# Layer 0: each group of four row transfers, from the fifth on, waits for one more convolution step

## The chip, the cores and the metric

The kernel runs on one core of a Trainium2 chip. The time is the device time of one execution, in microseconds (us). Of the kernel before there are three runs: median 1381.5 us, lowest 1380.76, highest 1385.48.

## What is computed

Four layers, each `x = x + attention(norm(x)) + ffn(norm(x))`, on x of 16 sequences x 256 tokens x 128 channels (4096 tokens). The change lies in layer 0, whose two parts are:

```
# attention part: a diagonal state-space scan, which is a causal convolution over time
y[b, t, d] = sum over s <= t of K[d, t - s] * xn[b, s, d]      K from log_A, B, C, D, log_dt
out_a      = xn + y @ W_out.T + b_out

# ffn part: a mixture of experts
probs      = softmax(norm(xf) @ gate_w.T)                      8 experts
w          = the two largest probs of each token, over their sum
out_f      = swiglu(xf, sWg, sWu, sWd)                         a shared expert, all tokens
           + sum over the two chosen experts e of w[e] * swiglu(xf, Wg[e], Wu[e], Wd[e])
swiglu(x, wg, wu, wd) = (silu(x @ wg) * (x @ wu)) @ wd
```

Layers 1 to 3 (two causal attentions with 16 heads, one windowed attention, three other feed-forward nets) are not touched.

## The kernel before

The work of an engine is a fixed program, written out by hand; engines wait for each other through counting semaphores. A layer ends with a barrier, so layer 1 starts when layer 0 is done. In layer 0 these pieces matter here:

- **The gate.** VectorE picks two experts for each token and works out `slot`: for choice n (0 or 1) and tile t (32 tiles of 128 tokens) the place of each token's row in the HBM array `expert_rows`, where the rows of one expert lie together. The array has two halves, for tiles 0 to 15 and 16 to 31.
- **The row transfers.** GpSimd (POOL) then issues 64 indirect DMAs from `send_rows` (L477), one for each tile and choice: 128 rows of `xn_tok`, 576 bytes each, go to their places. The order is: first half, choice 0 (16 transfers), then choice 1 (16), then the second half in the same way. Before choice 1 of a quarter (8 tiles) POOL waits for that quarter's choice 0 to have landed, moves the token numbers on (L473) and copies the second weight in (L474). Nothing else holds the transfers back: once `slots_ready` is there, POOL goes through all 64.
- **The convolution, beside it.** It has 16 steps of 8 channels. SyncE (SP) loads a step's Toeplitz matrices from HBM (`toeplitz`, L348, 1 MB) into one of four tiles; TensorE (PE) multiplies (`convolve`, L743 and L744, 32 matmuls, the last of which counts `c_mm` up by one); ScalarE (ACT) copies the result out of PSUM (`copy_y`, L572, which waits for `c_mm`); SP stores it (`store_y`, L353). A tile is loaded again for step s+4 only when `c_mm` says that step s is done.
- **The shared expert, beside it.** In the first 8 of the 16 steps PE also does one chunk of 512 tokens: `gate_up` (L708 to L710, 12 float16 matmuls), ahead of the convolution step, and `shared_down` (L726, 16 float32 matmuls) behind it. ACT does the silu (L558), VectorE (DVE) the product (L1067) and the sum into x (L1097). So a step is gate_up, convolve, shared_down in the first 8 steps, and convolve alone in the last 8.
- **The routed experts, after it.** When the convolution's results are stored, SP waits for the transfers of the first half (`wait_rows(0)`) and loads rows back, 512 at a time (a quad, L366); there are 20 quads. For each, PE turns the rows (L794), multiplies (L805 to L807, L726), and ACT scales the results (L606). POOL sends them with four indirect DMAs for each quad (`send_outs`, L492). The rows of the second half are waited for (`wait_rows(1)`) ahead of loading the eleventh quad.

The steps' waits on PE, and the loop of SP that follows them:

```
def convolve(step):
    a, w = step
    m = w % 2
    pe.wait_ge(t_in[w], a * 16 + 16)
    pe.wait_ge(u_taken, a * (2 * TW) + w * 2 + 2)
    pe.wait_ge(y_copied, a * TW + w + 1)

with sp.Fori(0, STEPS // TW - 1) as i:
    for m in range(TW):
        sp.wait_ge(c_mm, i * TW + m + 1)
        toeplitz((i + 1, m))
        store_y(i * TW + m, m % 2)
```

Of the kernel before, what the change touches and what calls it, by code (L numbers as in the profile page):

```python
# [17 lines left out]
TPC = CHUNK // P  # L18
# [121 lines left out]
HT = TILES // 2  # L140
# [30 lines left out]
def layer0(k, ctx):  # L171
# [92 lines left out]
    c_mm, y_copied, y_stored = k.sem("conv_mm"), k.sem("conv_y"), [k.sem(f"conv_stored{m}") for m in range(2)]  # L264
# [27 lines left out]
    with nc.Block() as block:  # L292
# [134 lines left out]
        def _(pool):  # L427
# [41 lines left out]
            def send_rows(n, quarter):  # L469
                at = slice(quarter * TILES // QUARTERS, (quarter + 1) * TILES // QUARTERS)  # L470
                if n:
                    pool.wait_ge(rows_sent[quarter], TILES // QUARTERS * 16)
                    pool.tensor_scalar(z[:, at, DM], z[:, at, DM], float(TOKENS), None, ALU.add).then_inc(id_moved, 1)  # L473
                    pool.tensor_copy(z[:, at, DM + 1], weight[:, 1, at]).then_inc(id_moved, 1)  # L474
                    pool.wait_ge(id_moved, 2 * quarter + 2)
                for t in range(at.start, at.stop):
                    pool.indirect_dma_start(rows_in, bass.IndirectOffsetOnAxis(ap=slot[:, n, t:t + 1], axis=0),  # L477
                                            z[:, t, :], None).then_inc(rows_sent[quarter], 16)

            for half in range(2):  # L480
                for n in range(2):
                    pool.wait_ge(slots_ready, n + 1)
                    for quarter in (2 * half, 2 * half + 1):
                        send_rows(n, quarter)
# [2026 lines left out]
```

## Time and profile before

| | |
|---|---|
| median of three runs | 1381.5 us |
| the profiled execution: its time, and its span | 1383.44 us, 1381.7 us |
| PE busy | 1129.3 us (82%) |
| DVE busy | 799.5 us (58%) |
| ACT busy | 616.9 us (45%) |
| POOL busy | 380.5 us (28%) |
| the 64 row transfers (L477), busy on POOL | 63.8 us |

The span is the time from the first to the last instruction of the profiled execution; 1.7 us of that execution lie outside it. The busy time of an engine is summed over stages that have different limits, so the table tells only that PE is the engine with most to do. Which wait matters in layer 0 is read from the timeline and the waits of that stage. Times in the timeline count from the start of the span. In a list of waits, the engine and its line stand ahead of the arrow and what released it behind; "issue" is time in which the engine waited for nothing that the profile shows; "remote" is a release for which the profile finds no instruction that ended just then.

### The profile page before, as it was taken

How to read it: one execution, taken by the hardware profiler on the slowest of the kernel's cores; microseconds unless marked ns; L12 is line 12 of the kernel's file. 1: busy time of each engine (PE TensorE's matmuls, PEld its weight loads, DVE VectorE, ACT ScalarE, POOL GpSimd, SP SyncE). 2: the span in 40 equal slices, each digit the busy share in tenths (PEclk: the TensorE clock that was granted, in tenths of full speed). 3: DMA queues.
4: the chain of work that ended last, by engine and by line, in shares of the span. 5: the costliest groups of instructions: out<-in, count | busy, mean ns of one | idle time of the engine just before them, and what ended most of it. 6: DMA issues, size and time to landing. Idle time of an engine off the chain costs nothing. (4 is left out here: it accounts for less than half of the span.)

```text
span 1381.7 us, 28274 instructions
## 1 busy us (share of the span) xinstructions
PE 1129.3 (82%) x9260; PEld 669.3 (48%) x9261; DVE 799.5 (58%) x1528; ACT 616.9 (45%) x1098; POOL 380.5 (28%) x504
## 2 busy tenths in 40 slices
PE   5551848878786799997996999999998499999696
PEld 2221527767643355554563555555545255555342
DVE  8520313333265688883457666666666488887344
ACT  5400213333242466665215555555555156666354
POOL 2377002554503244443503000000000044444102
PEclk9665898999997799999996999999999599999898
DMA  9541573344054233224300000000008132332002
GB/s 302 164 157 56 173 220 84 94 129 124 28 189 155 85 93 89 85 86 114 83 0 1 1 1 0 0 0 0 0 0 274 46 88 86 91 92 62 1 0 61
DMA packets 164846, 114.37 MB, mean 83 GB/s; under 512 B 16532, under 2 KB 157598, under 8 KB 164786
## 3 DMA queue, kind: packets, MB, share of 16 engines
q1 hardware_dynamic: 160178, 104.67, 25.3%
q0 software_dynamic: 4608, 8.93, 1.9%
q8 instruction: 34, 0.56, 0.2%
q14 instruction: 26, 0.21, 0.1%
HBM read 72.85 MB, written 37.55 MB: 80 GB/s over the span
## 5 line engine op out<-in xcount | busy, mean ns | idle before, releaser
L1645 DVE TENSOR_REDUCE at_mx<-banks 128x12 f32<-128x1536 f32 x128 | 225.1, 1759 | 82.9 <-PE banks L1513 80.2
L1629 ACT ACTIVATE at_p<-banks 128x512 f32<-128x512 f32 x384 | 213.9, 592 | 79.8 <-PE banks L1522 79.2
L1477 POOL TENSOR_SCALAR_AFFINE_SELECT at_p<-at_p 128x512 f32<-128x512 f32 x256 | 162.5, 636 | 255.3 <-ACT at_p L1629 252.7
L1522 PE MATMUL banks<-at_qbl,at_kst 128*128 128x512 f16 x384 | 129.8, 390 | 16.7 <-ACT at_p L1629 15.1
L492 POOL DMA_INDIRECT expert_outs<-ex_x_lo,rows_back_to x80 | 81.1, 1014 | 161.2 <-ACT ex_x_lo L606 142.2
L1067 DVE TENSOR_TENSOR ex_h_sb<-ex_sg,banks 128x512 f32<-128x512 f32 x56 | 38.4, 688 | 111.8 <-ACT ex_sg L558 42.6
L1468 POOL COPY at_va<-v_all 128x256 f32 (+1 forms) x32 | 12.7, 398 | 316.2 <-PEq L1496 316.2
L1879 PE MATMUL banks<-f_h_hi,w_hi_h 128*128 128x512 f16 x256 | 97.0, 379 | 0.0
L1880 PE MATMUL banks<-f_h_lo,w_hi_h 128*128 128x512 f16 x256 | 97.0, 379 | 0.0
L1881 PE MATMUL banks<-f_h_hi,w_lo_h 128*128 128x512 f16 x256 | 97.0, 379 | 0.0
L1532 PE MATMUL banks<-at_p,at_va 128*32 128x256 f32 x1024 | 85.4, 394 | 7.1 <-POOL at_p L1477 2.2
L726 PE MATMUL banks<-w_Wd,ex_h_sb 128*128 (+1 forms) x448 | 63.6, 293 | 32.7 <-issue 30.3
L1513 PE MATMUL banks<-mask_qk,ident 128*128 128x256 f16 x512 | 86.9, 297 | 0.0
L477 POOL DMA_INDIRECT expert_rows<-xn_tok,slot x64 | 63.8, 997 | 62.0 <-DVE slot L1038 42.9
L1509 PE MATMUL banks<-at_ksc,at_qst 32*128 32x128 f16 (+1 forms) x1024 | 47.4, 262 | 39.7 <-DVE at_mx L1645 30.0
L726 PEld LDWEIGHTS banks<-w_Wd,ex_h_sb 128*128 128x128 f32 x448 | 59.6, 208 | 37.1 <-issue 37.1
L1654 DVE COPY at_cx_sb<-banks 128x256 f32<-128x256 f32 x128 | 53.4, 417 | 22.5 <-PE banks L1533 22.5
L558 ACT ACTIVATE ex_sg<-banks 128x512 f32<-128x512 f32 x56 | 33.8, 605 | 72.9 <-remote 28.4
L1522 PEld LDWEIGHTS banks<-at_qbl,at_kst 128*128 128x128 f16 x384 | 36.8, 98 | 59.3 <-ACT at_p L1629 51.1
L1615 ACT ACTIVATE at_mT<-banks 16x256 f16<-16x256 f32 x32 | 11.9, 373 | 105.3 <-PE banks L1542 105.3
L1513 PEld LDWEIGHTS banks<-mask_qk,ident 128*128 128x128 f16 x512 | 42.2, 103 | 28.3 <-issue 23.2
L1533 PE MATMUL banks<-at_p,at_va 128*32 128x128 f32 x1024 | 55.3, 275 | 0.0
(394 smaller groups left out, 2362.5 us busy)
## 6 DMA issues: line engine op xcount, KB each, us to landing
xnT<-kernel_padded SPq DMA_DIRECT2D x8, 1024.0 KB
at_qst<-at_q_stacked SPq DMA_DIRECT2D x32, 256.0 KB, 3.0
at_ksc<-at_k_stacked SPq DMA_DIRECT2D x32, 256.0 KB, 3.3
at_kst<-at_k_stacked SPq DMA_DIRECT2D x32, 256.0 KB, 2.8
at_qbl<-at_q_stacked SPq DMA_DIRECT2D x128, 64.0 KB, 1.9
expert_rows<-ex_h_sb SPq DMA_DIRECT2D x1, 5760.0 KB, 17.9
gate_up_then_rows<-expert_rows SPq DMA_DIRECT2D x20, 260.0 KB, 3.0
ssm_powers<-kernel_padded SPq DMA_DIRECT2D x4, 1024.0 KB
```

Source lines behind the costliest of these rows:

```text
L477: pool.indirect_dma_start(rows_in, bass.IndirectOffsetOnAxis(ap=slot[:, n, t:t + 1], axis=0), z[:, t, :], None).then_inc(rows_sent[quarter ...
L492: pool.indirect_dma_start(rows_out, bass.IndirectOffsetOnAxis(ap=ids[:, r, b:b + 1], axis=0), ysc[:, r, b, :], None, bounds_check=2 * TOKE ...
L726: ins = pe.matmul(k.ps[:, OB[m], t * P:t * P + P], h[:, m, it, t * P:t * P + P], wd[:, sl(at, DM)], start=(it == 0), stop=(it == IT - 1), ...
L1477: pool.affine_select(out=blk, in_=blk, compare_op=ALU.is_ge, fill=0.0, base=0, pattern=[[0, 4], [1, P]], channel_multiplier=-1).then_inc(p ...
L1513: ins = pe.matmul(o, k.ident16[:], k.mask_qk[:, 0:2, :], start=False, stop=True, skip_group_check=True)
L1522: pe.matmul(o, kst[m][:, g, kt * P:kt * P + P], qbl[m][:, g, :, qt * P:qt * P + P], start=True, stop=True).then_inc(t_mm, 1)
L1532: pe.matmul(o, va[m][:, 0, 4 * g + j, :], p0[:, g, j, :], start=True, stop=False)
L1629: act.activation(dst, k.ps[:, T_B[(g * 3 + n) % 2], :].rearrange("p (j q) -> p j q", j=4), ACT.Exp, scale=scale).then_inc(p_ready, 1)
L1645: dve.tensor_reduce(mx[:, :, g * 4:g * 4 + 4].rearrange("p n j -> p j n"), k.ps[:, 0:4, 0:3 * P].rearrange("p j (n t) -> p j n t", t=P), A ...
L1879: pe.matmul(k.ps[:, bank, :], hi, x_hi, start=first, stop=False)
L1880: pe.matmul(k.ps[:, bank, :], hi, x_lo, start=False, stop=False)
L1881: return pe.matmul(k.ps[:, bank, :], lo, x_hi, start=False, stop=last)
```

## The change

Three lines are added in `send_rows`. The 64 transfers are counted in 16 groups of four, in the order in which POOL issues them (group 0 to 15). Groups 0 to 3 go as before. Ahead of the first transfer of group g, from group 4 on, POOL waits until `c_mm` is at least g - 3: group 4 for the first convolution step, group 5 for the second, and so on to group 15 for the twelfth.

```diff
                 for t in range(at.start, at.stop):
+                    group = (quarter // 2 * 2 * HT + n * HT + t % HT) // TPC
+                    if t % TPC == 0 and group > 3:
+                        pool.wait_ge(c_mm, group - 3)
                     pool.indirect_dma_start(rows_in, bass.IndirectOffsetOnAxis(ap=slot[:, n, t:t + 1], axis=0),
                                             z[:, t, :], None).then_inc(rows_sent[quarter], 16)
```

(HT is 16, TPC is 4.) The transfers, their order and their data are the same. The other four engines' programs are the same; their lines below the change have numbers that are higher by 3.

POOL's program from the second transfer to the middle of the first half's choice 1 and the start of the second half, before (`conv_mm` is the semaphore `c_mm`, `rows_sent0` counts landed transfers of a quarter, `id_moved` the two small operations):

```order
L477 DMA expert_rows<-xn_tok,slot 10240x144 x15
L473 TENSOR_SCALAR xn_tok<-xn_tok 128x8 [waits rows_sent0,slots_ready]
L474 COPY xn_tok<-gate_weight 128x8
L477 DMA expert_rows<-xn_tok,slot 10240x144 [waits id_moved]
L477 DMA expert_rows<-xn_tok,slot 10240x144 x7
L473 TENSOR_SCALAR xn_tok<-xn_tok 128x8 [waits rows_sent1]
L474 COPY xn_tok<-gate_weight 128x8
L477 DMA expert_rows<-xn_tok,slot 10240x144 [waits id_moved]
L477 DMA expert_rows<-xn_tok,slot 10240x144 x7
L477 DMA expert_rows<-xn_tok,slot 10240x144 [waits slots_ready]
L477 DMA expert_rows<-xn_tok,slot 10240x144 x15
```

The same stretch of POOL's program after the change:

```order
L480 DMA expert_rows<-xn_tok,slot 10240x144 x15
L473 TENSOR_SCALAR xn_tok<-xn_tok 128x8 [waits rows_sent0,slots_ready]
L474 COPY xn_tok<-gate_weight 128x8
L480 DMA expert_rows<-xn_tok,slot 10240x144 [waits conv_mm,id_moved]
L480 DMA expert_rows<-xn_tok,slot 10240x144 x3
L480 DMA expert_rows<-xn_tok,slot 10240x144 [waits conv_mm]
L480 DMA expert_rows<-xn_tok,slot 10240x144 x3
L473 TENSOR_SCALAR xn_tok<-xn_tok 128x8 [waits rows_sent1]
L474 COPY xn_tok<-gate_weight 128x8
L480 DMA expert_rows<-xn_tok,slot 10240x144 [waits conv_mm,id_moved]
L480 DMA expert_rows<-xn_tok,slot 10240x144 x3
```

A run of 8 or 16 transfers without a wait has become runs of four, each behind a wait on PE's count; the first 16 are as they were, and so are the two small operations and their place.

## Rows read from the trace of the kernel before

**Rows 1.** Stretches of layer 0: busy us and count of each engine, clock, DMA.
```profile
core 0: us, PE busy (x) PEld busy (x) DVE busy (x) ACT busy (x) POOL busy (x), PEclk, DMA share, GB/s
66.50:85.70 19.20, 8.11 (x24) 2.82 (x25) 6.26 (x5) 1.20 (x2) 15.28 (x16) 0.63 0.17 55
85.70:92.50 6.80, 6.32 (x39) 4.20 (x39) 0.56 (x3) 0.60 (x1) 5.24 (x7) 0.80 0.80 214
92.50:142.60 50.10, 11.76 (x33) 5.62 (x33) 2.42 (x5) 1.19 (x2) 34.91 (x40) 0.53 0.29 101
142.60:203.00 60.40, 44.24 (x559) 27.83 (x558) 18.63 (x46) 14.34 (x24) 0.00 (x0) 0.95 0.67 205
203.00:370.00 167.00, 131.49 (x1418) 119.80 (x1418) 60.27 (x126) 54.60 (x136) 73.24 (x72) 0.92 0.35 100
```
**Rows 2.** The row transfers as a group, and POOL's timeline (start us, us).
```profile
L477 POOL DMA_INDIRECT expert_rows<-xn_tok,slot x64: 954/959/2116, 51.8 to 137.3; - x64
...
77.37 0.96 POOL L477 DMA_INDIRECT expert_rows<-xn_tok,slot  x1 [0.31 <-issue]
...
82.42 2.12 POOL L477 DMA_INDIRECT expert_rows<-xn_tok,slot  x1 [0.30 <-issue]
...
86.67 1.07 POOL L477 DMA_INDIRECT expert_rows<-xn_tok,slot  x1 [0.28 <-POOL xn_tok L474]
```
**Rows 3.** PE's waits of 92.5 to 142.6 us: total us, times, longest.
```profile
PE banks L726 <- issue: 27.1, 14, 2.5
PE banks L743 <- issue: 6.0, 7, 1.5
PE banks L744 <- issue: 5.5, 5, 1.8
```
**Rows 4.** PE's timeline: the last matmul of convolution steps 2 and 3.
```profile
81.44 0.37 PE L744 MATMUL banks<-xnT,conv_u_now 128*16 128x128 f32 x1 [0.34 <-issue]
...
85.68 2.94 PE L726 MATMUL banks<-w_Wd,ex_h_sb 128*128 128x128 f32 x13 [0.34 <-issue]
...
110.31 0.37 PE L744 MATMUL banks<-xnT,conv_u_now 128*16 128x128 f32 x1 [1.76 <-issue]
```
**Rows 5.** ACT's timeline: result copies of steps 1, 2, 3, 4, 8, 12, 16.
```profile
62.22 0.60 ACT L572 ACTIVATE conv_ysb<-banks 128x512 f32<-128x512 f32 x1 [3.70 <-remote]
...
88.83 0.60 ACT L572 ACTIVATE conv_ysb<-banks 128x512 f32<-128x512 f32 x1 [10.33 <-remote]
...
143.46 0.60 ACT L572 ACTIVATE conv_ysb<-banks 128x512 f32<-128x512 f32 x1 [38.90 <-remote]
...
149.34 0.60 ACT L572 ACTIVATE conv_ysb<-banks 128x512 f32<-128x512 f32 x1 [1.55 <-PE banks L744]
...
173.42 0.60 ACT L572 ACTIVATE conv_ysb<-banks 128x512 f32<-128x512 f32 x1 [1.55 <-PE banks L744]
...
188.40 0.60 ACT L572 ACTIVATE conv_ysb<-banks 128x512 f32<-128x512 f32 x1 [4.19 <-DMA conv_out<-conv_ysb]
...
198.36 0.60 ACT L572 ACTIVATE conv_ysb<-banks 128x512 f32<-128x512 f32 x1 [2.43 <-DMA conv_out<-conv_ysb]
```
**Rows 6.** Timeline where the routed experts start: SP's loads, PE's first turn.
```profile
202.08 0.85 SPq L392 DMA_DIRECT2D conv_chunk<-conv_out  x2
203.03 6.95 SPq L366 DMA_DIRECT2D gate_up_then_rows<-expert_rows  x5
206.89 1.09 PE L794 MATMUL banks<-ident,gate_up_then_rows 128*128 128x128 f32 x4 [10.03 <-DMA gate_up_then_rows<-expert_rows]
```
**Rows 7.** Waits of 203 to 380 us, routed experts: total us, times, longest.
```profile
ACT ex_x_hi L598 <- remote: 35.5, 10, 4.1
...
ACT ex_x_lo L606 <- remote: 27.1, 10, 4.5
...
PEld banks L805 <- issue: 26.7, 26, 1.6
```
**Rows 8.** Instruction pages loaded in 92.5 to 142.6 us, by queue.
```profile
q0 software_dynamic: 1254, 2.88, 16.9%
...
q14 instruction: 1, 0.01, 0.0%
```

## The prediction

> **What bounds the kernel now.** The chain at the foot of the page covers only the last layer, so I read layer 0 from its stretches, then from timelines. Layers follow each other with barriers, so what layer 0 gains or loses the whole kernel does. Its routed part starts with loads at 202 to 203 us, and PE's first instruction there ends an idle time of 10.03 us whose release was that load [rows 6]. The load had waited for the convolution's results: the copy of step 16 is at 198.36 [rows 5]. So the end of the convolution sets the time here, and the row transfers do not: the last of the 64 is issued at 137.3 [rows 2], 66 us earlier.
>
> Next, how the steps follow each other. The reader is to see in [rows 5] that steps 4 to 8 are copied from 149.34 to 173.42, 6.0 us each, and steps 8 to 16 from 173.42 to 198.36, 3.1 us each, but that step 2 comes 26.6 us after step 1, and step 3 another 54.6 us later, with the same instructions in them. In the stretch 92.5 to 142.6, PE is busy 11.76 of 50.10 us with 33 matmuls, against 559 in the 60 us after it [rows 1], and all of its idle time, 38.6 us in 26 pieces, is put down to "issue", none to a semaphore or a transfer [rows 3]. At the same time its completions reach the others late: PE's last matmul of step 3 starts at 110.31 [rows 4], and ACT, free and waiting 38.90 us for it, goes at 143.46, its release "remote" [rows 5]; 33 us late. Step 2: 81.44 against 88.83, 7 us late.
>
> What goes with it is POOL. PE crawls from 66.5 to 85.7 and from 92.5 to 142.6 [rows 1]. POOL issues a transfer every 1.26 us (0.96 and 0.30 idle) from 51.8 on, with one real pause: after the one at 82.42 the next is at 86.67. PE is back to speed at 85.68 with 13 matmuls in 2.94 us [rows 4], and crawls again at 92.5, 5.8 us after POOL's restart. At the end POOL issues its last at 137.3 and is done at 138.3; PE runs freely from 142.6 on. So I read: a long unbroken row of indirect transfers holds up PE's completions and then its issue. It needs some time to set in (14.7 us from cold, 51.8 to 66.5; 5.8 after a short pause) and 3 to 4 us to go. That is an inference from coincidence; no row names the resource. The DMA engines are not it: in the first crawl they are busy 0.17 of the time [rows 1].
>
> **The change, part by part.** Added on POOL: 12 waits, on a count that PE raises anyway. No row shows the price of such a wait once it is met; by the idle 0.30 us that POOL has between any two transfers I bound it at 0 to 0.3 us each, and take nothing, since POOL has four steps of slack at its end. No instruction is added on PE, ACT, DVE or SP. Behind the waiting POOL stand only its own later transfers, and then the routed results' sends, of which the first is needed 20 us into the routed part. Group 15 waits for step 12 of 16.
>
> The sum, in times at which ACT copies a step, called S:
> - Groups 0 to 3 are as before, and group 4's step 1 has been copied at 62.22 before it is wanted. POOL stops after its 20th transfer, near 78.6 (the one at 77.37 is the 20th) [rows 2]. Crawl goes 3 us later, at 81.6, against 85.7 before. PE then has the rest of step 2's convolution to do: S2 near 84, not 88.8.
> - Step 3 is then an undisturbed 6.0 us plus 3 us of aftermath of group 5's burst: 9 us later, S3 near 93, not 143.5. This is the first large term: 50 us.
> - Steps 4 to 8 each let four transfers go, 4 x 1.26 = 5.0 us of POOL. The floor is the undisturbed 6.0 us a step. The ceiling is a burst wholly lost to PE plus 3 us until it is free: 5.0 + 3 + 6 = 14 us. The nearest row is the routed part, where POOL issues the same kind of transfer four to a quad, 72 in 167 us beside PE at 131.49 us busy [rows 1]: half of the 20 quads show "remote" waits, 3.6 us on ACT's copy [rows 7], and PE's own loss to "issue" is 1.3 us a quad (26.7 / 20). I take 7.5 us a step, a little above 6.0 + 1.3: S8 = 93 + 5 x 7.5 = 130.5, not 173.4.
> - Steps 9 to 12 without the shared expert: floor 5.0 us (POOL's four transfers; the steps themselves need 3.1), ceiling 5.0 + 3 + 3.1 = 11. Near the floor, as PE has little to do: 6 us. S12 = 154.5, not 188.4. Steps 13 to 16 have at most one burst beside them: 10.0 us as now [rows 5], S16 = 164.5, not 198.4.
>
> Gain: 33.9 us. The four transfers of group 15 end by 161, ahead of the routed loads at some 169, so `wait_rows` costs nothing, and if it came 5 us later only the second half's rows would be late, wanted at the eleventh quad. What is given back of the first two large terms (50 us at S3, 43 at S8) is just that transfers now lie beside steps 4 to 12, which ran undisturbed before. The profiled execution, 1383.44 us, becomes 1349.5; it lies 1.9 above the median of 1381.5, so against that median 1347.6, and I say 1348.
>
> Transfers now share the DMA engines with Toeplitz loads. The row: alone, at full rate, they take 0.17 of the engines, and the stretch 142.6 to 203 runs at 0.67 [rows 1]; together below 1, so I price this at nothing, with a bound of 17% of the 3.1 us steps, 0.5 us each, 2 us over steps 9 to 12. The Trainium skill (DMA: Bandwidth & Descriptors, on arbitration) has each DMA engine take turns between its queues, a packet at a time, which speaks against putting transfers beside loads. By that rule a load could be slowed more than by their share; at two queues taking equal turns four steps would lose up to 3.1 us each, 12 us, and the gain would be 22 us. No row here shows such a loss.
>
> **Rivals.**
> 1. *Every burst is lost to PE.* Place: steps 4 to 12, between POOL's release by `c_mm` and the next count. If the crawl, once warm, sets in at once and leaves 3 us after the burst, a step costs 14 and then 11 us: S8 = 163, S12 = 207, S16 = 217, 19 us slower, 1400. It decides from 5 x P1 + 4 x P2 = 95.4, which is 10.6 us a step on average. For it: at 92.5 only 5.8 us had passed since the restart. Against: those 5.8 us are longer than a burst, and the routed part, with bursts of four, keeps PE 79% busy.
> 2. *The crawl has another cause* and only coincides with POOL. Then S3 stays 143.5, POOL's transfers follow at 6 us a group, group 11 at 173.4 and the last near 199, still ahead of the routed loads: no change, 1381 to 1384. For it: no row names POOL as what PE waits for. Against: both ends of both crawls fit POOL's pauses, and "remote" waits of this length stand only where POOL sends. One such cause is instruction supply. The row: in 92.5 to 142.6 the queues show a single instruction page, on q14 [rows 8], while PE issued a matmul every 1.5 us throughout; a missing page would give one long gap. The Trainium skill (Runtime: NRT & Kernel Launch, on instruction fetch) says that a taken branch out of the pages at hand stalls an engine until the page is fetched; PE had just entered a loop. By that rule this rival's 1381 to 1384 would hold. The trace speaks against it: fetches are whole pages, and the second pass of the same loop ran freely.
> 3. *Half measure:* steps 4 to 8 take 10 us and steps 9 to 12 take 8, since a 1 us gap between bursts doesn't let the crawl drain. S16 = 93 + 50 + 32 + 10 = 185: 13 us faster, 1368.
>
> **How the numbers follow.** The forecast (7.5 and 6 us, with 6.0 and 5.0 from S3 = 91 as its lucky end: S16 = 151, 47 us faster, 1334) has 0.60; the half measure 0.20; no change 0.09; the slower one 0.11. Faster or slower than 0.3% (4 us, about what a measurement of this kernel can tell from none) is then 0.80 and 0.11. The range of 8 in 10 goes from 1334 to 1372: it takes in the lucky end and the half measure with some 4 us of contention, and leaves out rivals 1 and 2. The forecast's own range is 1334 to 1360.
>
> **What would show it.** Right: POOL's transfers in runs of four, the last between 155 and 175 us; S3 near 93; PE's "issue" time of L726, now 27.1 us in one stretch [rows 3], under 10 in all of the convolution; step copies 6 to 9 us apart up to S8; the routed loads start near 169 instead of 203, and everything behind is shifted by the same. Wrong: long "issue" gaps on PE after each burst with steps over 10.6 us (rival 1); S3 still over 130 (rival 2); or S16 as forecast but the routed part longer than its 167 us, if late second-half rows hold up quad 11.

## The result, and the profile after

The changed kernel takes 1342.62 us (median of 4 runs, 1341.66 to 1345.04) against 1382.93 of the kernel before, measured beside it (4 runs): a ratio of 0.971, 95% interval 0.969 to 0.973. It is 40 us faster. The profiled execution took 1342.36 us, its span is 1340.6.

One finding has to be told ahead of everything else, since the numbers below can't be read without it. The kernel before has two times, depending on when and where a group of runs is made: about 1382 us, as in the prediction's trace, or about 1285. Between 1292.5 and 1376.4 us no run of the kernel before lies. I call the first **condition X**, the second **condition Y**. The change gains 2.9% in X and nothing in Y. One execution of wait_only took 5313 us at a granted clock of 0.19, where its others took 1282 to 1287 at 0.92, and is left out of its ratio.

The changed kernel in X. ACT's timeline, copies of steps 2, 3, 4, 8, 9, 10, 11, 12, 13 and 16, which answer to [rows 5] (start us, us):

```profile
79.84 0.60 ACT L575 ACTIVATE conv_ysb<-banks 128x512 f32<-128x512 f32 x1 [5.27 <-remote]
...
92.14 0.60 ACT L575 ACTIVATE conv_ysb<-banks 128x512 f32<-128x512 f32 x1 [6.11 <-DMA conv_out<-conv_ysb]
...
96.28 0.60 ACT L575 ACTIVATE conv_ysb<-banks 128x512 f32<-128x512 f32 x1 [2.57 <-issue]
...
121.62 0.60 ACT L575 ACTIVATE conv_ysb<-banks 128x512 f32<-128x512 f32 x1 [1.55 <-PE banks L747]
127.86 0.60 ACT L575 ACTIVATE conv_ysb<-banks 128x512 f32<-128x512 f32 x1 [5.64 <-remote]
130.55 0.60 ACT L575 ACTIVATE conv_ysb<-banks 128x512 f32<-128x512 f32 x1 [2.09 <-PE banks L747]
140.07 0.60 ACT L575 ACTIVATE conv_ysb<-banks 128x512 f32<-128x512 f32 x1 [8.92 <-remote]
141.44 0.60 ACT L575 ACTIVATE conv_ysb<-banks 128x512 f32<-128x512 f32 x1 [0.78 <-PE banks L747]
150.78 0.60 ACT L575 ACTIVATE conv_ysb<-banks 128x512 f32<-128x512 f32 x1 [8.74 <-remote]
...
156.33 0.60 ACT L575 ACTIVATE conv_ysb<-banks 128x512 f32<-128x512 f32 x1 [1.33 <-DMA conv_out<-conv_ysb]
```

Step 16 is copied at 156.33 instead of 198.36, and step 3, whose copy came at 143.46, at 92.14. ("DMA conv_out<-conv_ysb" as a releaser means that the copy waited for an earlier result to be stored.) POOL's timeline in the same kernel, the ends and starts of some groups, which answers to [rows 2]:

```profile
76.47 0.96 POOL L480 DMA_INDIRECT expert_rows<-xn_tok,slot  x1 [0.31 <-issue]
80.08 2.00 POOL L480 DMA_INDIRECT expert_rows<-xn_tok,slot  x1 [2.65 <-remote]
...
88.31 1.07 POOL L480 DMA_INDIRECT expert_rows<-xn_tok,slot  x1 [1.88 <-PE banks L747]
...
128.51 1.07 POOL L480 DMA_INDIRECT expert_rows<-xn_tok,slot  x1 [1.27 <-remote]
...
137.45 0.96 POOL L480 DMA_INDIRECT expert_rows<-xn_tok,slot  x1 [0.30 <-issue]
...
149.66 0.96 POOL L480 DMA_INDIRECT expert_rows<-xn_tok,slot  x1 [0.30 <-issue]
```

The first 20 transfers go without a pause, as before. Of the groups behind them the reader is to see two kinds. Groups 4 to 11, of which the last transfer starts at 125.67, each end in a pause of 1.3 to 2.7 us until PE's count comes. From 128.51 to 137.45 eight transfers go without one, and again from 140.72 to 149.66: step 10 was there before group 12 had ended, so group 13 did not wait. ACT's two longest waits lie beside these two runs of eight, 8.92 and 8.74 us, "remote", for steps 11 and 13. The last matmuls of steps 9 and 11 on PE:

```profile
124.63 0.43 PE L747 MATMUL banks<-ssm_powers,conv_u_now 128*16 128x128 f32 x8
...
130.53 0.39 PE L747 MATMUL banks<-xnT,conv_u_now 128*16 128x128 f32 x2
```

Step 11 is copied 9.2 us after its last matmul. But step 9, beside group 11 with a pause ahead of it and behind it, is 2.8 us late too, and ACT waited 5.64 us for it: four transfers already touch PE a little. PE's waits of 80 to 128 us, which answer to [rows 3]:

```profile
PE banks L729 <- issue: 1.4, 3, 0.6
PE banks L747 <- issue: 0.8, 1, 0.8
PE banks L746 <- issue: 0.3, 1, 0.3
```

2.5 us of "issue" in 48 us, against 38.6 in 50 before. The loads that bound the routed part, after the change and, last, the end of it before:

```profile
161.00 7.15 SPq L366 DMA_DIRECT2D gate_up_then_rows<-expert_rows  x5
...
342.71 5.86 SPq L421 DMA_DIRECT2D gate_up_then_rows<-expert_outs  x8
```

```profile
381.80 5.39 SPq L421 DMA_DIRECT2D gate_up_then_rows<-expert_outs  x8
```

The routed part starts at 161.00 [rows 6: 203.03] and lasts until the loads of its results at 342.71, that is 181.7 us, against 178.8 before (203.03 to 381.80). So the span's 41.1 us are 42.0 from the start of the routed part, less 2.9 in it, and 2.0 behind it, which I did not follow.

### The profile page after: what moved, and what is told of

Read it like the earlier page. It is cut to its first block and busy times, and to the rows that moved or that the text cites. A ratio compares the mean times of both kernels' runs of the same rounds, so it can differ in the third digit from the quotient of the medians.

```text
span 1340.6 us, 28279 instructions
## 1 busy us (share of the span) xinstructions
PE 1126.8 (84%) x9260; PEld 667.2 (50%) x9261; DVE 799.0 (60%) x1528; ACT 616.6 (46%) x1098; POOL 379.3 (28%) x504
## 5 line engine op out<-in xcount | busy, mean ns | idle before, releaser
L1471 POOL COPY at_va<-v_all 128x256 f32 (+1 forms) x32 | 12.8, 399 | 316.1 <-PEq L1499 316.1
L729 PE MATMUL banks<-w_Wd,ex_h_sb 128*128 (+1 forms) x448 | 60.6, 292 | 13.8 <-DVE ex_h_sb L1070 10.8
```

The lines of the kernel that those rows point to most:

```text
L729: ins = pe.matmul(k.ps[:, OB[m], t * P:t * P + P], h[:, m, it, t * P:t * P + P], wd[:, sl(at, DM)], start=(it == 0), stop=(it == IT - 1), ...
```

## The experiments

**wait_only.** The added waits without the pauses:

```diff
-                        pool.wait_ge(c_mm, group - 3)
+                        pool.wait_ge(c_mm, 1)
```

Expected: 

> As the change, but every group from the fifth on waits for the first convolution step only, which is over before group 4 starts; so POOL has 12 more waits and no pause. Theory A (what slows PE is a long unbroken row of POOL's indirect transfers, and the change's gain comes from the pauses): as before, 1381 to 1385 us, step 3 copied near 143 us. Theory B (the wait instructions or the new places of POOL's instructions bring the gain): near 1343.

Measured: 1284.91 us against 1286.01 of the kernel before beside it, ratio 0.998 (0.997 to 1.000). Condition Y, on which neither expectation had counted. As a test of A against B it says nothing, and it was not run in X. Its trace says more, since its transfers are those of the kernel before, 64 without a pause from 50.9 to 136.5:

```profile
core 0: us, PE busy (x) PEld busy (x) DVE busy (x) ACT busy (x) POOL busy (x), PEclk, DMA share, GB/s
...
66.50:85.70 19.20, 14.14 (x126) 9.71 (x125) 7.73 (x16) 3.26 (x6) 15.02 (x18) 0.87 0.87 284
```

In the stretch where PE did 24 matmuls beside POOL's transfers in X [rows 1], it does 126 here. ACT's waits of 60 to 142 us:

```profile
ACT conv_ysb L575 <- DMA conv_out<-conv_ysb: 34.8, 9, 10.2
ACT ex_sg L561 <- PE banks L713: 16.3, 12, 2.9
ACT conv_ysb L575 <- PE banks L747: 9.3, 5, 2.9
ACT conv_ysb L575 <- issue: 1.6, 1, 1.6
```

No "remote" wait at all. ACT in the kernel before in X, 60 to 205 us:

```profile
ACT conv_ysb L572 <- remote: 52.9, 3, 38.9
ACT ex_sg L558 <- remote: 28.4, 4, 8.7
```

The copies of steps 8 and 16 in wait_only:

```profile
108.97 0.60 ACT L575 ACTIVATE conv_ysb<-banks 128x512 f32<-128x512 f32 x1 [1.55 <-PE banks L747]
...
137.51 0.60 ACT L575 ACTIVATE conv_ysb<-banks 128x512 f32<-128x512 f32 x1 [3.87 <-DMA conv_out<-conv_ysb]
```

So a long row of transfers holds PE up in X only. The routed part (loads at 142.13 and 286.12) takes 144 us here and 179 in X, and the parts behind differ by 3 us in all: almost all of the 97 us between the conditions lies in the two parts in which POOL sends by index. That the routed part's own sends cost its 35 us is inferred from this; no run takes them away.

**pause, eights, tail**, in the same group of runs, so in Y too. Their edits:

```diff
# pause: no wait on c_mm; in its place
+                        for m in range(4):
+                            pool.memset(idle[:], 0.0).then_inc(idle_set, 1)
+                            pool.wait_ge(idle_set, 4 * (group - 4) + m + 1)
# eights
-                    if t % TPC == 0 and group > 3:
+                    if t % TPC == 0 and group > 3 and group % 2 == 0:
# tail
-                        pool.wait_ge(c_mm, group - 3)
+                        pool.wait_ge(c_mm, {12: 10, 13: 12, 14: 14, 15: 16}.get(group, group - 3))
```

Expected of pause: 

> No wait on PE's count; in its place, ahead of each group from the fifth on, POOL writes four times to a tile that nobody reads, with a wait behind each, some 2 to 2.5 us of pause per group, about what the change's waits last. Theory A (pauses alone): steps 4 to 8 at 6.5 to 8 us each as with the change, convolution over near 150 to 165, 1340 to 1355 us. Theory C (a pause helps only where it lasts until PE's completions have come through, which the wait on the count ensures and a fixed time does not): the crawl sets in again after some groups, 1355 to 1380 us.

Expected of eights: 

> As the change, but only the even groups from the fifth on wait, so transfers go in runs of eight (10 us) with the same count reached at each run's start. Theory A (length of the unbroken run decides; sets in 5 to 6 us after a short pause): each run costs PE some 5 us of crawl and 3 us of aftermath, 6 runs, two of which the change already has in the last steps: 4 more x 8 = 30 us less gained at most, 10 at least: 1352 to 1373 us. Theory D (only the average rate of transfers counts, 64 over 100 us): as the change, 1341 to 1346.

Expected of tail: 

> As the change, but groups 12 to 15 wait for steps 10, 12, 14 and 16 instead of 9, 10, 11 and 12, so that no two groups follow each other without a pause in the last eight steps, where the trace of the change shows two runs of eight with 8.9 and 8.7 us of late completions. Theory A: these two waits go, steps 9 to 16 take 3.1 to 4 us each, convolution over 8 to 14 us earlier, and the rows of the second half are wanted only later: 1329 to 1337 us. Rival (the last groups end after the convolution and the routed part waits for them, or the crawl there comes from the loads' share of the DMA engines): 1341 to 1350.

Measured: 1285.38 us, ratio 0.999 (0.998 to 1.001); 1285.12, 0.999 (0.997 to 1.000); 1286.32, 1.000 (0.998 to 1.002). None moved; none of the expectations was tested. eights was not tried in X, so theory D, that only the average rate of transfers counts, stays open there. (Against theory B speaks behind, below: POOL's program has an added wait there, at the change's place, and the crawl comes wherever the transfers go.)

**after_again.** The changed kernel, to see whether the condition or the kernel makes the difference.

Expected: 

> The changed kernel once more, since the first four experiments ran on a chip on which the kernel before takes 1286 us and PE's completions come on time beside the transfers. Theory E (the crawl of PE beside the transfers belongs to the chip or its surroundings, not to the program alone): where the kernel before takes about 1286 us the change makes no difference within 0.3%; where it takes about 1382 the ratio is 0.971 again, and no time lies between. Theory F (the change gains wherever it runs, and the first four experiments merely lacked it): 0.97 on either.

Measured: 1283.32 us against 1283.54, ratio 1.000 (0.998 to 1.002). Theory E stands in its first half, theory F falls. (The place E gave, "the chip", is wrong: see the last section.)

**behind.** In condition X (the kernel before beside it: 1382.99).

```diff
-                    if t % TPC == 0 and group > 3:
-                        pool.wait_ge(c_mm, group - 3)
+                    if t % TPC == 0 and group == 4:
+                        pool.wait_ge(c_mm, STEPS)
```

Expected: 

> All 48 transfers from the fifth group on wait for the sixteenth and last convolution step, so nothing is sent beside steps 3 to 16. Where PE crawls beside transfers (kernel before near 1382 us): theory A expects steps 4 to 8 at 6.0 us and 9 to 16 at 3.1, step 16 copied near 150 instead of 198. Where it does not (kernel before near 1285): step 16 is copied 2 to 5 us earlier than the 137.5 us seen beside transfers, since they then take no share of the DMA engines. In both, POOL's 48 transfers take 60 us after step 16, the first half's rows are there 20 us late and the results' sends queue behind the second half's transfers: routed part 20 to 60 us longer, 1300 to 1345 us where the kernel before takes 1285.

Measured: 1380.51 us, ratio 0.998 (0.996 to 0.999). ACT's copies of steps 2, 5, 8 and 16, with no transfer between 73 and 145 us:

```profile
76.94 0.60 ACT L575 ACTIVATE conv_ysb<-banks 128x512 f32<-128x512 f32 x1 [0.90 <-PE banks L747]
...
102.90 0.60 ACT L575 ACTIVATE conv_ysb<-banks 128x512 f32<-128x512 f32 x1 [1.64 <-PE banks L747]
...
120.87 0.60 ACT L575 ACTIVATE conv_ysb<-banks 128x512 f32<-128x512 f32 x1 [1.55 <-PE banks L747]
...
146.02 0.60 ACT L575 ACTIVATE conv_ysb<-banks 128x512 f32<-128x512 f32 x1 [2.43 <-DMA conv_out<-conv_ysb]
```

Steps 5 to 8 take 6.0 us, steps 9 to 16 3.1, and step 16 is copied at 146.02 as expected (150). This is the direct proof in X: without the transfers the crawl is gone from the same loop. Beside transfers in Y steps 9 to 16 took 28.5 us (108.97 to 137.51), without them 25.2 here: 0.4 us a step, the most that the transfers' share of the DMA engines can cost there, if the two conditions differ in nothing else. The 52 us of gain left nothing in the total. The two loads that bound the routed part:

```profile
167.38 6.17 SPq L366 DMA_DIRECT2D gate_up_then_rows<-expert_rows  x5
...
382.51 5.99 SPq L421 DMA_DIRECT2D gate_up_then_rows<-expert_outs  x8
```

The routed part starts 21 us after step 16, instead of 5, since the first half's rows come late, and takes 215 us instead of 179. The expectation had the results' sends queue on POOL behind transfers. That is not what happened: the transfers end at 207.7, and POOL then waits another 14.1 us for the first results. What is slow is PE, which crawls again, now in the routed part. Its stretch beside the transfers, ACT's wait there, and POOL's first send of results:

```profile
167.40:208.00 40.60, 11.34 (x66) 8.39 (x66) 2.69 (x8) 1.79 (x3) 30.76 (x35) 0.54 0.33 99
```

```profile
200.64 0.60 ACT L601 ACTIVATE ex_x_hi<-banks 128x512 f16<-128x512 f32 x1 [21.87 <-remote]
```

```profile
221.77 0.99 POOL L495 DMA_INDIRECT expert_outs<-ex_x_lo,rows_back_to  x1 [14.10 <-ACT ex_x_lo L609]
```

66 matmuls in 40.6 us, where the kernel before does 334 in the first 41 us of its routed part. The first send comes 54 us after the part's first load instead of 21, and this is nearly all of the 36 us that the part is longer. So the crawl followed the transfers to another place and to other matmuls, a second sign beside its absence from the convolution.

**direct.** In the same group of runs, X. Plain DMAs in place of the indirect ones, in the old order without added waits. The rows then lie in token order and not by expert, so the output is another one, and the run is read for its time only:

```diff
-                    pool.indirect_dma_start(rows_in, bass.IndirectOffsetOnAxis(ap=slot[:, n, t:t + 1], axis=0),
-                                            z[:, t, :], None).then_inc(rows_sent[quarter], 16)
+                    block_at = (quarter // 2 * HALF_BLOCKS + n * HT + t % HT) * P
+                    pool.dma_start(rows_in[block_at:block_at + P, :], z[:, t, :]).then_inc(rows_sent[quarter], 16)
```

Expected: 

> The 64 transfers are plain DMAs of the same tiles to the next free places of the same array instead of indirect ones, so the experts compute on rows in token order (the output is another one; the same number of rows and bytes moves). No added waits. POOL still makes the descriptors. Theory G (what PE suffers from is POOL's descriptor traffic, indirect or not): where the kernel before takes 1382 us this one does too. Theory H (it is the scattered 576-byte rows in HBM): the crawl is gone or shorter there, below 1350. Where the kernel before takes 1285, both expect 1275 to 1290.

Measured: 1323.58 us (2 runs) against 1382.99, ratio 0.957 (0.955 to 0.960). POOL's timeline and ACT's copy of step 16:

```profile
69.38 12.78 POOL L478 DMA_DIRECT2D expert_rows<-xn_tok  x24 [0.29 <-POOL xn_tok L474]
...
89.25 4.32 POOL L478 DMA_DIRECT2D expert_rows<-xn_tok  x8 [0.30 <-POOL xn_tok L474]
```

```profile
139.62 0.60 ACT L572 ACTIVATE conv_ysb<-banks 128x512 f32<-128x512 f32 x1 [3.68 <-DMA conv_out<-conv_ysb]
```

Here POOL sends the same bytes more than twice as fast (0.53 us each, 24 in 12.78), in a run of 24 without a pause, beside steps 3 and 4, and PE does not crawl: it does 95 matmuls in those 12.8 us, and its waits from 50 to 142 us hold no "issue". So neither the bytes, nor their rate, nor a long row of DMAs from POOL as such is what holds PE up. Theory G falls. What is left of the causes named here is the indirect form or the scattered rows; the run changes both at once, and can't say which. The routed part (144.29 to 326.13) still takes 182 us, with its 80 indirect sends: the time of X and not of Y.

**pause_2 and tail_2**, then **tail_3**, **pause_3** and **pause_4**: the same two kernels, to meet condition X.

Expected of pause_2: 

> The kernel of the run named pause once more, for a chip on which the kernel before takes about 1382 us. Theory A (pauses of 2 us in the row of transfers are enough, whatever they are tied to): 1340 to 1355 us. Theory C (a fixed pause is too short where completions have piled up; the wait on PE's count lets them through): 1355 to 1380. Where the kernel before takes about 1285: no difference, as in the first run.

Expected of tail_2: 

> The kernel of the run named tail once more, for a chip on which the kernel before takes about 1382 us. Theory A (the two runs of eight transfers in the last eight steps cost the change 8.9 and 8.7 us of late completions; spaced out they go): step 16 copied 8 to 14 us earlier than the 156.3 us of the change, 1329 to 1337 us. Rival (they cost nothing on the path, or the last groups now end after the convolution and hold up the routed part): 1341 to 1350. Where the kernel before takes about 1285: no difference.

Expected of tail_3: 

> The same kernel as tail and tail_2, which both met chips without the crawl. Where the kernel before takes about 1382 us: theory A (the two runs of eight transfers in the last eight steps are what is left of the crawl in the change) expects step 16 copied 8 to 14 us ahead of 156.3 us and 1329 to 1337 us; the rival (no cost on the path, or the last groups end late) 1341 to 1350. Where it takes about 1285: no difference for a third time, which would leave this open.

Expected of pause_3: 

> The kernel of pause and pause_2, which both met conditions without the crawl. Where the kernel before takes about 1382 us: theory A (pauses of 2 us in the row of transfers are enough, whatever they are tied to) expects 1340 to 1355 us; theory C (a fixed pause is too short where completions have piled up, while the wait on PE's count lets them through first) 1355 to 1380. Where it takes about 1285: no difference.

Expected of pause_4: 

> The same kernel a last time, for the condition that pause, pause_2 and pause_3 missed. Kernel before near 1382 us: theory A (fixed pauses of 2 us are enough) 1340 to 1355 us, theory C (the wait on PE's count is needed) 1355 to 1380. Kernel before near 1285: no difference, and it stays open whether a fixed pause would do.

| | us | kernel before beside it | ratio | condition |
|---|---|---|---|---|
| pause_2 | 1284.88 | 1285.12 | 1.000 (0.999 to 1.002) | Y |
| tail_2 | 1287.04 | 1285.12 | 1.001 (0.999 to 1.002) | Y |
| tail_3 | 1338.01 | 1383.32 | 0.968 (0.965 to 0.970) | X |
| pause_3 | 1286.23 | 1285.69 | 1.001 (0.999 to 1.003) | Y |
| pause_4 | 1337.66 | 1380.35 | 0.968 (0.963 to 0.972) | X |

tail_3: ACT's waits from 116 to 160 us, with the last groups spaced out:

```profile
ACT conv_ysb L575 <- DMA conv_out<-conv_ysb: 18.1, 6, 6.5
ACT conv_ysb L575 <- remote: 6.5, 2, 5.6
```

The change has 23.3 us of "remote" waits on this copy from 116 to 165, tail_3 6.5, of which 5.6 are for step 9; but step 16 is copied at 152.16, only 4.2 us earlier, since stores of the results then hold the copies up, step 11 by 6.5 us and steps 12 to 14 to 3.7 us each. That the long waits go with the two runs of eight is as theory A had it; the forecasts of A (8 to 14 us, 1329 to 1337) were both missed, and 1338.01 us lies between A and its rival. Its ratio's interval touches that of the change (0.969 to 0.973), and they were not run side by side: 4 us better is likely, not shown.

pause_4: POOL's timeline with fixed pauses, and ACT's copies of steps 3 and 16:

```profile
90.17 2.27 POOL L481 MEMSET idle<- 128x512 f32 x4
92.73 1.07 POOL L483 DMA_INDIRECT expert_rows<-xn_tok,slot  x1 [0.28 <-POOL idle L481]
...
96.62 0.96 POOL L483 DMA_INDIRECT expert_rows<-xn_tok,slot  x1 [0.30 <-issue]
97.57 2.30 POOL L481 MEMSET idle<- 128x512 f32 x4
```

```profile
90.83 0.60 ACT L578 ACTIVATE conv_ysb<-banks 128x512 f32<-128x512 f32 x1 [9.29 <-DMA conv_out<-conv_ysb]
...
151.60 0.60 ACT L578 ACTIVATE conv_ysb<-banks 128x512 f32<-128x512 f32 x1 [1.65 <-DMA conv_out<-conv_ysb]
```

A pause of 2.3 us after every four transfers, tied to nothing, gives all of the change's gain (ratio 0.968 against 0.971): the pauses suffice, as theory A has it, and theory C falls. The time is 2 us under A's range. Completions were not all on time: ACT still waited 5.42 us, "remote", for step 5, and 5.95 for step 9. The wait on the convolution is only a way of making pauses, and near the end of the convolution, where steps are shorter than a group, it makes none.

## Why the prediction was right, point by point

- **The bound.** That the convolution's end sets the start of the routed part held: 4.7 us from step 16 to the first load of rows both before and after.
- **The cause.** I took it from coincidence that an unbroken row of indirect transfers holds up PE. behind and pause_4 show it in X. What I did not see is that it needs a condition that no row of one trace can show. Rival 2 (another cause, 1381 to 1384) is false in X, but its outcome, no gain, is what happens in Y. That the change was measured in X was luck: four of eight groups of runs were in Y.
- **How the crawl sets in.** I had read 5.8 us after a short pause, longer than a group of four. In the change's trace step 9 slows about 3 us after group 11's start (121.86; from 124.85 PE's matmuls come one or two at a time). Pauses work although a group does touch PE.
- **Step 2, step 3.** Forecast 84 and 93; copied at 79.84 and 92.14, and step 3's count had reached POOL by 88.31. The term of 50 us was 51.3.
- **Steps 4 to 8.** Forecast 7.5 us each, S8 = 130.5. Measured 121.62. From group 7's start (94.52) to group 11's (121.86), which are step 4's and step 8's counts, it is 6.8 us a step: this term was priced 0.7 us too high. The copies stand 4.1, 5.0, 6.7, 6.9 and 6.7 us apart, the first two less since step 3's copy had waited for a store.
- **Steps 9 to 12.** Forecast 6 us each, measured 5.0 (121.62 to 141.44). That this meets the "floor" of 5.0 is luck. POOL waits for PE, not PE for POOL, so POOL's four transfers (5.0 us) are no floor for a step. The four steps took 6.2, 2.7, 9.5 and 1.4 us, long where completions came late.
- **Steps 13 to 16.** Here the sum failed the other way. "At most one burst beside them: 10.0 us as now" took 14.9 (141.44 to 156.33). Groups 14 and 15 went as one run of eight from 140.72, and step 13 came 9.3 us after step 12. I had named a pause of 1 us as perhaps too little to drain (rival 3), and had not asked where there would be none. It is the same slip as the floor: steps of 3.1 us outrun groups of 5.0, the count is there already, and POOL doesn't wait. So the last transfer started at 149.66, before the 155 to 175 us that I had named as a sign of being right.
- **Steps 1 to 16 together.** S16 forecast 164.5, measured 156.33: the gain was 42.0 where 33.9 was summed. Up to S12 the forecast was 13.1 us late, and the last term takes 4.9 back. The total, 1342.6 against a forecast of 1348, is 5 us off, inside the forecast's own range, and partly by errors of opposite sign.
- **Rival 1** (each burst lost, 14 us a step) is refuted by 6.8. **Rival 3** (half measure, 1368) too.
- **The DMA engines' share.** Bound of 0.5 us a step in steps 9 to 12; 0.4 measured between wait_only and behind, across the two conditions, and within X at most 0.5 (steps 9 to 16 took 29.3 us in tail_3, 25.2 in behind), what is left of the crawl included. The Trainium skill's rule on taking turns between queues (DMA: Bandwidth & Descriptors, on arbitration), by which I had allowed up to 3.1 us a step, did not show at that size.
- **Given back.** I priced the routed part at no change; it took 2.9 us more.

## What to carry to other kernels

Idle time that a profile puts to "issue" on TensorE, together with "remote" releases on the engines behind it, went here with completions of TensorE that came late; look then for what another engine does at just those times. Indirect transfers from GpSimd in a long row can be that. A pause of some 2 us after every four of them took 3.2% off in X and cost nothing measurable in Y; it did not bring X down to Y's time, 1338 against 1285 us. A plain DMA where the addresses are known may do more (1323.58 us in X, with another output). Moving the row behind the stage that suffers only moves the crawl, as behind shows. A wait on another engine's count makes a pause only where that engine is the slower one. And repeat a comparison at another time before a stall of this kind is called a property of the program: here the whole gain depends on a condition under which the kernel was first measured.

## What the runs showed of the hardware that was not expected

- One kernel, two times: 1380 to 1383 us in four groups of runs, 1283.5 to 1286 in four. Chip 4 served both, and so did chip 2, at most some 20 minutes apart. It is thus not a property of the chip alone. What it is stays open.
- In X, completions of PE arrived up to 33 us late beside a row of 40 transfers, 8 and 9 us late beside 8, and mostly within 1 us beside 4 with a pause behind (2.8 us for step 9 in the change, 4.0 for step 5 in pause_4). Beside the row of 40 PE's issue slowed to one matmul in 1.5 us. Which resource the two share was not found. GpSimd's plain DMAs of the same rows, at 0.53 us each instead of 1.26, bring no such lateness.
- The crawl is not bound to the convolution's loop: in behind it came beside the 48 late transfers in the routed part, 66 matmuls in 40.6 us.
- In Y the routed part, with its 80 indirect sends, takes 144 us instead of 179. That the sends make this difference is likely, not shown.
